# Output projection of a post-norm block, computed transposed from products of rounded parts

## What is computed

```python
q = einsum('bse,hed->bhsd', x, Wq) + bq        # 16 heads of 64; k and v likewise
scores = where(causal, q @ k.T / sqrt(64), -inf)
out = (softmax(scores) @ v)                    # heads side by side: (b, 256, 1024)
x = layernorm(x + out @ Wo + bo)
# mixture of experts: 8 experts, the best 2 per token by softmax(logits / 1.5)
xn = layernorm(x) * gamma + beta
y = sum over the two of gate * (silu(xn @ W1[e]) @ W2[e])
x = layernorm(x + y)
```

## Time and profile before

| | |
|---|---|
| runs | 1309.6, 1308.0, 1307.06 us; median 1308.0 |
| the profiled execution | span 1306.0 us from first to last instruction; its own time outside the span isn't listed, the median lies 2.0 us above |
| busy | TensorE 1284.0 us, VectorE 1098.7, ScalarE 1078.0, GpSimd 508.6 |
| attention sequences | until about 1004 us, then the experts |

### The profile page before, as it was taken

How to read it: one execution, slowest core, us unless ns; L and a number is a source line. 1 busy time by engine, 2 the same in 40 slices (tenths; PEclk the granted TensorE clock), 3 DMA queues, 4 the chain that set the end, 5 groups by cost and what they waited for, 6 DMA issues and landing times.

```text
span 1306.0 us, 36164 instructions
## 1 busy us (share of the span) xinstructions
PE 1284.0 (98%) x11298; PEld 1139.8 (87%) x11298; DVE 1098.7 (84%) x5201; ACT 1078.0 (83%) x3481; POOL 508.6 (39%) x1075
## 2 busy tenths in 40 slices
PE   7999999999999999999999999999999999999997
PEld 6888888888888888888888888888887999999983
DVE  6888888888888888888888888888887898888847
ACT  7888888888888888888888888888887777777737
POOL 1024333333333333333333333333333676565645
PEclk9999999999999999999999999999999999999999
DMA  5000100100000000000000000000023687777749
GB/s 212 18 22 30 34 30 33 34 32 14 14 14 14 14 14 14 14 14 15 14 14 14 14 14 18 17 16 16 16 110 125 178 236 232 232 232 228 223 133 338
DMA packets 58860, 98.19 MB, mean 75 GB/s; under 512 B 9376, under 2 KB 36131, under 8 KB 58416
## 3 DMA queue, kind: packets, MB, share of 16 engines
q1 hardware_dynamic: 49024, 78.67, 19.3%
q0 software_dynamic: 8640, 17.13, 3.8%
q10 hardware_dynamic: 1008, 0.08, 0.1%
HBM read 65.85 MB, written 30.91 MB: 74 GB/s over the span
## 4 chain that ended last, share of the span: by engine, by line
PE 91%; DVE 3%; ACT 2%; DMA 1%; issue 1%; SPq 0%; POOL 0%; POOLq 0%; ACTq 0%; DVEq 0%
PE ps_f L1116 16%; PE ps_b L1150 14%; PE ps_a L1116 14%; PE ps_s L1157 13%; PE ps_s L1138 10%; PE ps_s L1116 7%; PE ps_a L1348 4%; PE ps_b L1348 4%; PE ps_s L1141 4%; PE ps_s L1418 2%; PE ps_a L1190 1%; PE ps_f L1182 1%; PE ps_s L1162 1%; ACT probs L608 1%; DMA m_x<-queue 1%
## 5 line engine op out<-in xcount | busy, mean ns | idle before, releaser
L608 ACT ACTIVATE probs<-probs,neg_max 128x256 f32<-128x256 f32 x512 | 255.4, 499 | 128.7 <-DVE neg_max L859 128.7
L855 DVE CUSTOM_DVE_ANT_0 probs<-ps_s,mask 128x256 f32<-128x256 f32 x512 | 214.4, 419 | 32.1 <-PE ps_s L1141 29.7
L474 POOL TENSOR_SCALAR ln_b<-mv 128x2 f32<-128x2 f32 x32 | 6.0, 188 | 500.6 <-DVE mv L922 500.6
L1157 PE MATMUL ps_s<-ident,probs 128*128 128x128 f32 x1536 | 199.7, 274 | 0.0
L610 ACT ACTIVATE probs<-probs,neg_max 128x128 f32<-128x128 f32 x512 | 198.7, 388 | 0.0
L1150 PE MATMUL ps_b<-pt,f_y 128*64 128x256 f32 (+1 forms) x2048 | 194.7, 332 | 1.6 <-issue 0.9
L869 DVE TENSOR_SCALAR probs<-probs,inv_sums 128x256 f32<-128x256 f32 x512 | 182.3, 356 | 9.1
L573 POOL DMA_INDIRECT y_tok<-f_y,m_dest x142 | 145.7, 1026 | 84.2 <-DVE m_dest L1022 57.6
L1150 PEld LDWEIGHTS ps_b<-pt,f_y 128*64 128x64 f32 x2048 | 131.6, 137 | 51.4 <-issue 6.7
L1138 PE MATMUL ps_s<-qk 64*128 64x256 f32 x1024 | 170.6, 409 | 5.0 <-ACT qk L598 1.9
L1157 PEld LDWEIGHTS ps_s<-ident,probs 128*128 128x128 f32 x1536 | 172.3, 142 | 0.4 <-issue 0.3
(11 more groups left out here) (208 smaller groups left out, 3151.1 us busy)
## 6 DMA issues: line engine op xcount, KB each, us to landing
m_w<-w_split SPq DMA_DIRECT2D x71, 512.0 KB
m_x<-queue SPq DMA_DIRECT2D x71, 133.0 KB
f_y<-y_tok SPq DMA_DIRECT2D x32, 256.0 KB, 6.3
queue<-empty SPq DMA_DIRECT2D x8, 532.0 KB
x_raw<-in_x SPq DMA_DIRECT2D x32, 128.0 KB, 2.1
w_split<-f_y SPq DMA_DIRECT2D x8, 512.0 KB, 2.6
out_x<-f_y SPq DMA_DIRECT2D x16, 256.0 KB, 6.5
y_tok<-f_y,m_dest POOLq DMA_INDIRECT x142
```

What stands on the lines that cost most here:

```text
L608: act.activation(row[:, 0:2 * P], row[:, 0:2 * P], ACT.Exp, scale=-1.0, bias=neg_max[:, pair, h, 0:1], accum_out=sums[:, d % 2, pair, h, 0:1])
L855: dve.tensor_tensor_reduce(out=row[:, 0:2 * P], in0=ps_s[:, pair, h, 0:2 * P], in1=mask[:].rearrange("p a b -> p (a b)"), scale=-1.0, scal ...
L1157: ins = pe.transpose(ps_s[:, pair, h, dst:dst + P], probs[:, buf, pair, h, src:src + P], ident[:])
```

## The change

The projection is computed transposed: Wo is stationary, the outputs move, and the result has channels on partitions and the 256 tokens as columns. Both operands are split into an fp32r value and an fp32r rest, and three products (high by high, high by rest, rest by high) are summed, 24 matmuls of 256 columns per sequence. ScalarE writes the rounded outputs `ot_hi` in place of the plain copy; VectorE computes the rests `ot_lo` by a subtraction from `ps_b`; GpSimd splits Wo once at the start. ScalarE then copies the result to `out_t`, TensorE transposes it back in two transposes, and VectorE adds the residual for both tiles in one instruction.

The orders move with it. TensorE: the transposes of the next input from q2 to q1, the first half of the projection at the end of q1, its second half in q2 before the q/k projection; in q2 the ranks before the transposes of pair 0, and the q/k projection of pair 1 at the end of the step. `attention_output` now waits for `ot_lo_done` of the step before. ScalarE: the copy of the outputs always stands between the exponentials of pair 1 and `evacuate_qk` of pair 0. VectorE: the rest of x in q1, the places (from the ranks) before the second normalisation, `second_pt` before it in q1, both statistics in q2. `probs` takes the place of `ot` in the shared tile. GpSimd's token sends stand at the head of the next q0 instead of the end of q3, behind the same instructions as before.

```diff
-        ot = early_use[:, 3 * HD:3 * HD + 2 * PAIRS * S].rearrange("p (a c t) -> p a c t", a=2, c=PAIRS)
+        probs = early_use[:, 3 * HD:6 * HD].rearrange("p (a b h t) -> p a b h t", a=2, b=2, h=2)
...
+        wo_hi = sb("wo_hi", [P, PAIRS, D], F32R)
+        wo_lo = sb("wo_lo", [P, PAIRS, D], F32R)
+        ot_hi = sb("ot_hi", [P, PAIRS, S], F32R)
+        ot_lo = sb("ot_lo", [P, PAIRS, S], F32R)
+        out_t = sb("out_t", [P, S])
...
-        def projection_at(n, i):
-
-            return ps_f[:, 0:D] if n < SEQS else ps_f[:, i * D:(i + 1) * D]
+        def projection_at():
+
+            return ps_f[:, S:S + TILES * D].rearrange("p (i d) -> p i d", i=TILES)
...
+            def split_projection():
+                pool.wait_ge(wo_loaded, 16)
+                pool.tensor_copy(wo_hi[:], wo_sb[:]).then_inc(wo_hi_done, 1)
+                pool.wait_ge(wo_hi_done, 1)
+                pool.tensor_tensor(wo_lo[:], wo_sb[:], wo_hi[:].bitcast(F32), ALU.subtract).then_inc(wo_lo_done, 1)
...
+                if q == 0 and n - 1 in LATE:
+                    send_tokens(n - 1)
...
-                if q == 3 and n in LATE:
-                    send_tokens(n)
...
             def copy_outputs(d):
-                par, first = (d - 2) // QUADS % 2, (d - 2) % QUADS * 2
+                n, first = (d - 2) // QUADS, (d - 2) % QUADS * 2
                 act.wait_ge(o_ready, d - 1)
-                act.activation(ot[:, par, first:first + 2, :].rearrange("p c t -> p (c t)"), ps_b[:], ACT.Copy
-                               ).then_inc(ot_done, 1)
+                if n >= 1:
+                    act.wait_ge(out_half_ready, 2 * n - (1 if first < 4 else 0))
+                act.activation(ot_hi[:, first:first + 2, :].rearrange("p c t -> p (c t)"), ps_b[:], ACT.Copy
+                               ).then_inc(ot_hi_done, 1)
+
+            def copy_projection(n):
+                act.wait_ge(out_half_ready, 2 * n)
+                if n >= 2:
+                    act.wait_ge(proj_ready, n - 1)
+                act.activation(out_t[:], ps_f[:, 0:S], ACT.Copy).then_inc(out_t_done, 1)
+
+            def round_input(n):
+                act.wait_ge(xt_ready, n + 2)
+                act.activation(xt_hi[:, (n + 1) % 2, :], ps_f[:, 0:S], ACT.Copy).then_inc(xt_hi_done, 1)
...
-                if d >= 2 and q in (1, 2):
-                    copy_outputs(d)
-                if q == 2 and n + 1 < SEQS:
-                    act.wait_ge(xt_ready, n + 2)
-                    act.activation(xt_hi[:, (n + 1) % 2, :], ps_f[:, 0:S], ACT.Copy).then_inc(xt_hi_done, 1)
-                if q == 2 and n == SEQS - 1:
-                    evacuate_second_v(n * 4 + 4, 1)
+                if q == (1 if n >= 1 else 2) and n + 1 < SEQS:
+                    round_input(n)
                 if d == LAST - 1:
                     copy_outputs(d)
                 if d < LAST:
                     for h in range(2):
                         exponentials(d, 1, h)
+                if q == 2 and n in MID:
+                    copy_projection(n)
...
-                if d >= 2 and q == 0:
+                if 2 <= d < LAST - 1:
                     copy_outputs(d)
...
-                if 2 <= d < LAST - 1 and q == 3:
-                    copy_outputs(d)
...
+            def rest_of_outputs(d):
+                first = (d - 2) % QUADS * 2
+                dve.wait_ge(ot_hi_done, d - 1)
+                dve.tensor_tensor(ot_lo[:, first:first + 2, :].rearrange("p c t -> p (c t)"), ps_b[:],
+                                  ot_hi[:, first:first + 2, :].bitcast(F32).rearrange("p c t -> p (c t)"),
+                                  ALU.subtract).then_inc(ot_lo_done, 1)
+
...
+            def statistics(n):
+                dve.wait_ge(res_done, n)
+                for i in range(TILES):
+                    ins = dve.bn_stats(stats[:, i, :], res[:, i, :])
+                ins.then_inc(stats_done, 1)
+
+            def variance(n):
+                dve.wait_ge(stats_done, n)
+                if n >= 2:
+                    dve.wait_ge(z_done, n - 1)
+                for i in range(TILES):
+                    ins = dve.bn_aggr(mv[:, i, :], stats[:, i, :])
+                ins.then_inc(mv_done, 1)
 
...
-            def residual(n, i):
-                dve.wait_ge(proj_ready, (n - 1) * TILES + (i + 1 if n < SEQS else TILES))
-                if i == 0:
-                    dve.wait_ge(xb_done, n)
-                    if n >= 2:
-                        dve.wait_ge(z_done, n - 1)
-                dve.tensor_tensor(res[:, i, :], projection_at(n, i), xb[:, i, :], ALU.add).then_inc(res_done, 1)
+            def residual(n):
+                dve.wait_ge(proj_ready, n)
+                dve.wait_ge(xb_done, n)
+                if n >= 2:
+                    dve.wait_ge(z_done, n - 1)
+                dve.tensor_tensor(res[:], projection_at(), xb[:], ALU.add).then_inc(res_done, 1)
...
-                if n in MID:
-                    variance(n, q)
+                if q == 3 and n in MID:
+                    variance(n)
...
+                if q == (1 if n >= 1 else 2) and n + 1 < SEQS:
+                    if n == 0:
+                        rest_of_xt(2, 1)
+                    else:
+                        rest_of_xt(n + 2, (n + 1) % 2)
...
                 if q == (3 if n < SEQS - 1 else 1):
                     evacuate_first_v(n * 4 + 3, 1)
+                if q == 2 and n in LATE:
+                    places(n)
                 if d == LAST - 1:
+                    rest_of_outputs(d)
+                if d == LAST - 1 or (q == 1 and n in MID):
                     second_pt(d)
                 if d < LAST:
                     normalise(d, 1)
-                if 1 <= d < LAST - 1:
+                if q == 2 and n in MID:
+                    residual(n)
+                    second_pt(d)
+                    statistics(n)
+                if 2 <= d < LAST - 1:
+                    rest_of_outputs(d)
+                if 1 <= d < LAST - 1 and (q in (0, 3) or n == 0):
                     second_pt(d)
                 if SEQS - 2 <= n and d < LAST - 1:
                     first_table(d - (SEQS - 2) * QUADS)
                 if q == 0 and n in LATE:
                     router_difference(n)
-                if q == 2 and n in LATE:
-                    places(n)
-                if q in (1, 2) and n in MID:
-                    residual(n, q - 1)
...
+            def first_transposes(d):
+                pe.wait_ge(probs_done, d * 2 - 1)
+                pe.wait_ge(max_done, min(d * 4 + 2, LAST * 4))
+                transpose_probs((d - 1) % 2, 0).then_inc(pt_first_ready, 1)
...
+            def output_projection(n, half):
+                for c in range(half * PAIRS // 2, (half + 1) * PAIRS // 2):
+                    if c % 2 == 0:
+                        pe.wait_ge(ot_lo_done, (n - 1) * QUADS + c // 2 + 1)
+                    for k, (lhs, rhs) in enumerate(split_terms(wo_hi[:, c, :], wo_lo[:, c, :],
+                                                               ot_hi[:, c, :], ot_lo[:, c, :])):
+                        ins = pe.matmul(ps_f[:, 0:S], lhs, rhs, start=(c == 0 and k == 0),
+                                        stop=(c == PAIRS - 1 and k == 2))
+                ins.then_inc(out_half_ready, 1)
+
+            def transpose_projection(n):
+                pe.wait_ge(out_t_done, n)
+                for i in range(TILES):
+                    ins = pe.transpose(projection_at()[:, i, :], out_t[:, i * P:(i + 1) * P], ident[:])
+                ins.then_inc(proj_ready, 1)
...
-                if q == 2 and n + 1 < SEQS:
+                if q == (1 if n >= 1 else 2) and n + 1 < SEQS:
                     if n == 0:
                         pe.wait_ge(bo_done, 1)
                     else:
-                        pe.wait_ge(res_done, n * TILES - 1)
+                        pe.wait_ge(v_done, n * 4 + 2)
                     pe.wait_ge(x_loaded[(n + 1) % 2], ((n + 1) // 2 + 1) * 16)
...
+                if q == 2 and n in MID:
+                    if n == SEQS - 1:
+                        pe.wait_ge(v_done, n * 4 + 4)
+                        output_projection(n, 0)
+                    output_projection(n, 1)
                 if q == 3 and n < SEQS - 1:
...
+                if q == 1 and 1 <= n < SEQS - 1:
+                    if n == 1:
+                        pe.wait_ge(wo_lo_done, 1)
+                    pe.wait_ge(xt_lo_done, n + 2)
                     output_projection(n, 0)
...
-                        if pair == 1 and q == 3 and n in LATE:
-                            pe.wait_ge(ranks_done, n - 1)
...
-                        pe.wait_ge(ot_done, d - 2)
+                        pe.wait_ge(ot_lo_done, d - 2)
...
+                if q == 2 and n in LATE:
+                    pe.wait_ge(r_diff_done, n - 1)
+                    pe.wait_ge(chosen_any_done, n - 1)
+                    pe.wait_ge(max_done, d * 4 + 4)
+                    ranks(n)
```

(16 more changed lines are left out.)

77 lines of the change are left out of this document (28 added, 49 removed).

## The result

The changed kernel takes 1320.3 us (median of 4 runs, 1318.6 to 1320.7), the kernel before 1307.9 (4 runs on the same chip, 1307.1 to 1309.6). The ratio is 1.0089, 95% interval 1.0074 to 1.0103: slower by 12.5 us. The profiled execution took 1320.66, its span is 1318.9, so 1.8 us lie around the span.

A forecast was written before the change was run, and what follows sets the result against it. TensorE bounds the kernel now; after the change, VectorE's q1 and q2 turns and ScalarE's q3 chain lengthen each sequence by 0.38 us. 29 x 0.38 = 11, less about 1, on about 1308 gives 1318 us, range 1296 to 1331.

The forecast's parts named there:

- the likeliest case: Whole kernel: the forecast's own case, slower at 1311 to 1324 us, chance 0.45.
- TensorE's list: TensorE alone, per sequence: steps of about 7.6, 7.7, 7.5 and 7.7 us, sum 30.6, a gain of 0.44.
- VectorE's turns: VectorE in q1 and q2: turns of 8.1 and 8.0 us, each with a 0.61 us subtraction; in time again in q0.
- The 6.66 us on ScalarE: ScalarE in q3: from VectorE's first maximum to the pt copy's end, 6.13 us plus output copy and hand-over.
- What sets q3's maxima: VectorE's turns of q1 and q2: q3 starts at 0.97 + 8.1 + 8.0 = 17.07 us, 0.8 late.
- The ranks and their additions, moved ahead of the normalisation, fit into the wait before it: VectorE in q2, before the second normalisation: this work was claimed to fit into the wait for ScalarE's exponentials.
- q3's own stall swallows it: ScalarE's q/k evacuation of q2 ends about 0.1 us after TensorE wants the next pair-1 scores; claimed covered.
- In q0 only: Sign: TensorE idle before pair-0 scores, put down to ScalarE's pt copy, about 0.5 us or more per sequence, only there.
- The sum: Whole kernel: 29 sequences x 0.38 = 11 us, less about 1, so +10 on about 1308: 1318 us.
- the two ends: Sequence 1 (no router turn) and sequence 31 (no x to prepare): about 1 us less.
- Rival 1: Whole kernel: TensorE stays the bound, 31 x 0.44 = 14 us faster, 1294 us; chance 0.25.
- Rival 3: VectorE's later turns: contention, with GpSimd busiest in q3, adds 6 to 17 us more, 1324 to 1335; chance 0.20.

The follow-up runs named there:

- all_short: Changed kernel with ScalarE's rounded copy and VectorE's subtraction both cut to 16 of 512 columns in every step from sequence 1 on; 1301.9 us.
- rest_short_q1: Changed kernel with VectorE's subtraction in step q1 alone cut to 16 of 512 columns from sequence 1 on; nothing gained, no exact time given.
- two_products: Changed kernel without the third product (rounded outputs with Wo's rest), 8 matmuls less per sequence; 0.10 us of 0.94 shows in the period.
- move_q1q2: Changed kernel, whole: q2's ranks ahead of both q/k projections, two small router pieces into VectorE's waits of q1 and q3; a miss, no time given.
- move_both: Changed kernel with q1/q2 moves, plus q3's ScalarE output copy behind its pt copy and VectorE's pt copy before its subtraction; nothing to speak of changed.
- move_all: move_both with VectorE's subtraction of q2 also ahead of the residual addition, nothing left out; 1315.5 us, period 31.31.
- short_both_q3: Changed kernel with ScalarE's rounded copy and VectorE's subtraction both cut to 16 of 512 columns in step q3 alone; 1309.6 us.

## Why the prediction was right, and where it was not

The forecast was 1318, slower; it came to 1320.3, in the likeliest case. By its own steps:

**TensorE's list: right.** Forecast 7.6, 7.7, 7.5, 7.7 us. all_short has 7.61, 7.71, 7.57 (7.84 less the 0.27) and 7.68. In the chain the projection groups are 1.42 us in q1, as said, and 1.63 in q2. Those 0.2 are no cost of the group: from the first product's start to the last one's it takes 1.39 us in q1 (585.98 to 587.37) and 1.41 in q2 (590.70 to 592.11). The chain counts a piece from the end of the one before, and the records of transposes reach further into the group behind them (to 586.23) than those of the attention outputs (to 590.77).

**VectorE's turns: right in length, q2's in part by luck.** 8.04 and 7.90 us against 8.1 and 8.0. Behind q2's second normalisation the pieces take 2.33 us (594.56 to 596.89) where I had 2.52, statistics and residual above all; in front of it stands the wait for the ranks, which I had at nothing. The subtraction is 0.59 to 0.60 from start to start against 0.61. In q0 VectorE is in time again. The Trainium skill, "VectorE: DVE Perf Modes", section "The DRAIN you can't avoid", says that the next operation doesn't start before the pipe is empty; the row has 0.67 us and the next start after 0.59. The same section adds that an operation that isn't held starts earlier, which the prediction left out and these rows agree with.

**The 6.66 us on ScalarE: right within 0.1.** 596.89 to 603.51 with 0.14 to the scores, 6.76 in all; the hand-over that I had at 0.05 is 0.14. q0's scores come 23.67 us after q1's, forecast 23.7. The copy belongs in that chain: without it the scores came earlier, though VectorE then held pair 1.

**What sets q3's maxima: wrong as the only path.** The step reads: "if VectorE starts q1 in time ... it starts q3 at 0.97 + 8.1 + 8.0 = 17.07 us". It does start there, at 16.91, but VectorE's q1 turn can be shortened by 0.3 us without effect (rest_short_q1). The sentence that failed is "The ranks and their additions, moved ahead of the normalisation, fit into the wait before it". The last piece of ScalarE's exponentials and VectorE's normalisation in the changed kernel:

```profile
593.09 0.19 ACT L627 ACTIVATION_READ_ACCUMULATOR f_y<-f_y,neg_max 128x1 f32 x1
```

```profile
593.43 0.17 DVE L891 RECIPROCAL inv_sums<-sums 128x4 f32<-128x4 f32 x1
```

The ranks end at 593.24 us, 13.26 after q1's scores, and the additions behind them keep VectorE to 593.43. By the 0.22 us of two_products the normalisation could have begun at 593.31 without them. So the path that I summed, VectorE's q1 turn with ScalarE's exponentials, ends 0.12 us ahead of TensorE's list up to the ranks, and the 0.10 per sequence that two_products gained is that distance. A third path, TensorE's transposes of pair 1, ends within 0.1 us of VectorE's copy of pt. The number was right, and partly by luck: pieces priced 0.19 too long stood in for a path that was missing. The remedy that it suggests (shorten q1's turn) was not right.

**ScalarE's chain in q1: missed.** The prediction applied it to q3 alone. The same sum in q1 is 0.97 + 6.64 + 0.15 = 7.76, above TensorE's 7.6, and that is the step in every kernel that keeps the copy whole in q1, while all_short has 7.61. It made the path to the ranks 0.15 us longer.

**"q3's own stall swallows it"** (the q/k evacuation) held only while the stall was there. In the changed kernel q3's pair-1 scores wait 0.14 us for it. The wait is 0.27 in rest_short_q1, move_q1q2 and move_both, where it costs nothing, because the path to q0's scores runs over VectorE; in all_short and move_all it is on the chain.

**"In q0 only"**, about the gaps: the marked waits for ScalarE's copy of pt sum to 12.3 us in 33 cases, the 0.3 us of q0's scores; the two of about 0.1 in q1 and q2 are in none of the wait rows.

**The sum: right by errors that partly cancel.** The forecast sequence was 31.43 us, 0.38 above the 31.05 walked; the same four steps are now 31.34 (579.98 to 611.32), 0.29 more. Of the 0.09 between them, q3's maxima came 0.16 earlier than forecast and q0 is 0.03 shorter, ScalarE's chain 0.10 longer. The mean period, 31.42, looks like the forecast 31.4, but it has to be set against the mean of 31.12 that the earlier trace rows give: 29 x 0.307 = 8.9 us, not 11. And the two ends cost 4.0 us where I had them gain 1. Ahead of the first reduction it is 1.3. Of the 2.7 behind the last, 1.7 lie in front of the first matmul on `m_x`, the experts' input, most of it a late DMA (TensorE waits 2.55 us for `m_x` until 1014.75; before, 1.10 until 1002.81). The other 1.0 lies in the experts' part, 304.2 us against 303.2, which takes from 301.0 to 305.3 in the kernels of the study, in no order that follows their edits. Why the DMA is later no run took apart, and it stays open.

Rival 1 (TensorE stays the bound) failed for the reason given, and its size was right: with the two costs cut, TensorE's list is 30.6 if the 0.27 are taken off. Rival 3's scaling of 128x128 at 0.48 to 0.49 us comes once per sequence in both kernels, so it adds nothing; whether GpSimd stretches it no run tested.

## What to carry to other kernels

When a kernel is tuned so far that the three busiest engines run at 83 to 98%, walk every step's chain on every engine, not only the one that looks late, and list for each wait the next two that end within 0.1 to 0.2 us of it: removing one shows the next, and a cut that gains nothing alone (short_both_q3 against its parts) may be half of one that gains all. Ask of added work not how long it is but which side of the engine's last wait it stands on; of four equal subtractions, one cost 11 us and the other three about nothing when cut by themselves. A sum that comes out right doesn't show that its path is the one that counts: cutting a piece of it does. A copy that releases a PSUM buffer delays the other engine by its place in the queue, even when its own result isn't needed for long.
